# The local term of a Runge-Kutta step's first stage in two halves, with one prepared row between the two sums

## The chip, the cores and the metric

The kernel runs on one core of a Trainium2 chip. The metric is the device time of one execution in microseconds, the median of several executions. Of the engines, TensorE (PE in the profile, its weight loads PEld), VectorE (DVE) and ScalarE (ACT) carry the work; GpSimd (POOL) and the DMA queues have little to do.

## The reference

A sequence model in two parts. A recurrence with 256 time steps makes one state vector `q` of 512 values for each of 8 batch rows; each step is a classic four-stage Runge-Kutta step whose derivative holds a cube and a 512 x 512 product. The trace of `q` then goes through a gated feed-forward network with 4-bit weights, is normalised, and is added to the input.

```python
def _derivative(q, p, drive, coupling, bias):
    i_couple = jnp.tanh(q) @ coupling.T
    dq = q - q ** 3 / 3.0 - p + drive + i_couple + bias
    dp = EPSILON * (q + ALPHA - BETA * p)
    return (dq, dp)

def _rk4_step(q, p, drive, coupling, bias):
    dq1, dp1 = _derivative(q, p, drive, coupling, bias)
    dq2, dp2 = _derivative(q + 0.5 * DT * dq1, p + 0.5 * DT * dp1, drive, coupling, bias)
    dq3, dp3 = _derivative(q + 0.5 * DT * dq2, p + 0.5 * DT * dp2, drive, coupling, bias)
    dq4, dp4 = _derivative(q + DT * dq3, p + DT * dp3, drive, coupling, bias)
    ...

w_gu = _dequant_fp4(gate_up_packed, gate_up_scales, GROUP_SIZE)
w_down = _dequant_fp4(down_packed, down_scales, GROUP_SIZE)
gate_up = jnp.einsum('bsh,oh->bso', x, w_gu)
gate, up = (gate_up[..., :I], gate_up[..., I:])
h = jax.nn.silu(gate) * up
y = jnp.einsum('bsi,hi->bsh', h, w_down)
rms = jnp.sqrt(jnp.mean(y * y, axis=-1, keepdims=True) + EPS)
return y / rms
```

## The kernel before

The 512 values of `q` lie as 128 partitions x 4 chunks x 8 batch rows, so an operation on all of `q` has 32 elements in each partition and one on half of it (chunks 0 and 1, or 2 and 3) has 16. The 256 steps are cut into 16 blocks of 16 steps. A block's four stages per step make 64 stages; `s` counts them, and `s % 4` is the stage within the step (0 to 3).

One stage is a loop through four engines, written out by hand and held together by semaphores alone:

- ScalarE (L558, L560) makes the hyperbolic tangent of each half of the stage's `q` twice, once rounded to 16 bits (`th`) and once in 32 bits (`t32`, in the profile `t`): four instructions, half 0 first.
- VectorE (L592, `low_part`) subtracts the two, which gives the low 16 bits of `th`. I call the two of a stage low 0 and low 1.
- TensorE (L520) runs 32 matmuls of `th` with the coupling weights. The first 4 wait for half 0 of the rounded tangent, the 9th for half 1 (`tanh_hi`), the 13th for low 0 and the 21st for low 1 (`tanh_lo`). The 24th signals `first_half`, the 32nd `second_half`.
- VectorE makes `q_sq` (L596) and `q_cub` (L599), and from them the local term, which is all of the derivative that needs no product. `local_in` (L604) writes it into two of the six slots of the PSUM tile `scan_ps`: one slot belongs to half 0 of the sum, one to half 1. The other four slots are TensorE's. `finish` then sums three slots for each half (L628 and L630, which I call sum 0 and sum 1), and gives the next stage's `q`. ScalarE starts the next stage as soon as sum 0 is done.

The local term of stage `i` uses a row that is linear in the earlier stages' values. These rows are built up ahead by `add_q` and `add_p` (L586): `with_q1[0]` is used in stage 1, `with_q1[1]` goes into `with_q2[0]` late in stage 1, for stage 2. VectorE's queue is in order, so each of these stands at a fixed place between the others:

```python
                local_in(s)
                add_q(with_q1[1], 2, BY_Q1, q1, with_p[:, 2])
                finish(s)

                s = 4 * t + 1
                ffn_part(s)
```

The feed-forward network of a block is computed during the block behind it. A plan (`Schedule`) gives TensorE 132 products (L297 and L309, in the trace two records each) over the 64 stages: two behind each stage's 32 matmuls, but three behind stage 0 of the steps 0, 4, 8 and 12. VectorE has the network's element-wise work only at the head of a stage 1 (`ffn_part`): in a full block `ffn_h32` (L325) in the steps 0, 2, 3, 5, 6, 8, 9, 10, 12, 13 and 15, a third of `norm_out` (L346) in the steps 4, 7 and 11, and nothing in the steps 1 and 14. Block 0 has no network beside it, and block 1 has 10 of the `ffn_h32` (not that of step 0) and no `norm_out`. The last block's network runs in a tail behind the recurrence.

Of the kernel before, what the change touches and what calls it, by code (L numbers as in the profile page):

```python
# [21 lines left out]
ALU = mybir.AluOpType  # L22
# [8 lines left out]
HC = KT // 2  # L31
# [34 lines left out]
BY_R, BY_P, BY_Q1, BY_Q2, BY_Q3, BY_Q4, BY_ONE = range(7)  # L66
# [30 lines left out]
UNIT = [1.0] + [row_unit(i) for i in range(1, ROWS)]  # L97
# [103 lines left out]
def program(nc, x, drive, cond_t, coupling_t, bias_t, packed, scales, out):  # L201
    ctx = ExitStack()

    def sb(name, shape, dt=F32):
        return ctx.enter_context(nc.sbuf_tensor(name, shape, dt))
# [4 lines left out]
    with ctx:  # L210
# [12 lines left out]
        q_cub = sb("q_cub", [P, KT, B])  # L223
# [3 lines left out]
        with_p = sb("with_p", [P, ROWS, KT, B])  # L227
        with_q1 = [sb(f"with_q1_{i}", [P, KT, B]) for i in (1, 2, 3)]
# [33 lines left out]
        local_ps = scan_ps[:, 2 * APART:4 * APART].rearrange("p (h r) -> p h r", h=2)[:, :, 0:HB]  # L262

        def halves(tile):

            return tile.rearrange("p (h c) b -> p h (c b)", h=2)
# [306 lines left out]
        def dve_block(dve, now, before, ffn, rest):  # L573

            linear = [with_p[:, 0], with_q1[0][:, :, :], with_q2[0][:, :, :], with_q3[:, :, :]]
            count = [0]

            def local(ins):

                count[0] += 1  # L580
                ins.then_inc(now.local, 1)
                return count[0]

            def add(to, x, factor, base):

                return local(nc.vector.scalar_tensor_tensor(to, x, factor, base, ALU.mult, ALU.add))  # L586

            def low_part(s, half):

                c = slice(half * HC, (half + 1) * HC)  # L590
                dve.wait_ge(now.tanh_32, 2 * s + 1 + half)
                nc.vector.tensor_tensor(th[s % 2][:, c, 1, :], t32[:, c, :], th[s % 2][:, c, 0, :],  # L592
                                        ALU.subtract).then_inc(now.tanh_lo, 1)

            def square(i, q):
                return local(nc.vector.scalar_tensor_tensor(q_sq[:, :, :], q, CUBE[i], q, ALU.mult, ALU.mult))  # L596

            def cube(i, q):
                return local(nc.vector.scalar_tensor_tensor(q_cub[:, :, :], q_sq[:, :, :], OWN[i], q,  # L599
                                                            ALU.add, ALU.mult))  # L600

            def local_in(s):
                i = s % 4
                nc.vector.scalar_tensor_tensor(local_ps, halves(linear[i]), UNIT[i], halves(q_cub[:, :, :]),  # L604
                                               ALU.mult, ALU.add).then_inc(now.first_half, 1)

            def add_p(step, first, rows):
                p_rows = p_state[:, :, :].unsqueeze(1).to_broadcast([P, rows, KT, B])
                return add(with_p[:, first:first + rows], p_rows, P_ALL, sum_r[:, step % STEPS, first:first + rows])

            def add_q(to, row, column, q, base):
                return add(to[:, :, :], q, float(BY[row, column]), base)

            def clip(to, signal):
                nc.vector.tensor_scalar(to, q_raw[:, :, :], -CLAMP * S, CLAMP * S, ALU.max, ALU.min).then_inc(signal, 1)

            def ffn_part(s):

                for job in jobs(now, before, ffn, rest, s):
                    dve_ffn(dve, *job)  # L620

            def finish(s):

                i = s % 4
                q_next = q_raw if i == 3 else q_stage[i]

                dve.wait_ge(now.first_half, 2 * s + 2)
                nc.vector.tensor_reduce(q_next[:, 0:HC, :], three[0], AX.X, ALU.add).then_inc(now.q_ready, 1)  # L628
                dve.wait_ge(now.second_half, s + 1)
                nc.vector.tensor_reduce(q_next[:, HC:KT, :], three[1], AX.X, ALU.add).then_inc(now.q_ready, 1)  # L630

            for t in range(STEPS):
                q1 = hist[now.parity][:, :, t - 1, :] if t else hist[1 - now.parity][:, :, STEPS - 1, :]
                q2, q3, q4 = (x[:, :, :] for x in q_stage)

                s = 4 * t
                if t == STEPS - 1 and before:
                    dve.wait_ge(now.other_cleared, 1)
                if t == 0 and before:
                    dve.wait_ge(before.local, LOCALS)  # L640
                add_p(t, 1, 2)
                if t == 1 and rest:
                    dve.wait_ge(before.gu_ready, UNITS)
                if t:
                    dve.wait_ge(now.q_ready, 2 * s)
                    clip(q1, now.clipped)
                elif before:
                    dve.wait_ge(before.q_ready, 2 * STAGES)
                    clip(q1, before.clipped)
                low_part(s, 0)  # L650
                if t:
                    dve.wait_ge(now.clipped, t)
                elif before:
                    dve.wait_ge(before.clipped, STEPS)
                squared = square(0, q1)
                low_part(s, 1)
                dve.wait_ge(now.local, squared)
                cubed = cube(0, q1)
                add_q(with_q1[0], 1, BY_Q1, q1, with_p[:, 1])
                dve.wait_ge(now.local, cubed)  # L660
                local_in(s)
                add_q(with_q1[1], 2, BY_Q1, q1, with_p[:, 2])
                finish(s)

                s = 4 * t + 1
                ffn_part(s)
                dve.wait_ge(now.q_ready, 2 * s)
                squared = square(1, q2)
                low_part(s, 0)
                dve.wait_ge(now.local, squared)  # L670
                cubed = cube(1, q2)
                low_part(s, 1)
                dve.wait_ge(now.local, cubed)
                local_in(s)
                add(p_part[0][:, :, :], p_state[:, :, :], P_SUM[0], q1)
                add_q(with_q2[0], 2, BY_Q2, q2, with_q1[1][:, :, :])
                row3 = add_p(t, 3, 1)
                finish(s)

                s = 4 * t + 2  # L680
                dve.wait_ge(now.local, row3)
                add_q(with_q1[2], 3, BY_Q1, q1, with_p[:, 3])
                dve.wait_ge(now.q_ready, 2 * s)
                squared = square(2, q3)
                low_part(s, 0)
                dve.wait_ge(now.local, squared)
                cubed = cube(2, q3)
                low_part(s, 1)
                dve.wait_ge(now.local, cubed)
                local_in(s)  # L690
                p2 = add(p_part[1][:, :, :], p_part[0][:, :, :], P_SUM[1], q2)
                with_23 = add_q(with_q2[1], 3, BY_Q2, q2, with_q1[2][:, :, :])
                dve.wait_ge(now.local, p2)
                add(p_part[2][:, :, :], p_part[1][:, :, :], P_SUM[2], q3)
                finish(s)

                s = 4 * t + 3
                dve.wait_ge(now.local, with_23)
                add_q(with_q3, 3, BY_Q3, q3, with_q2[1][:, :, :])
                dve.wait_ge(now.q_ready, 2 * s)  # L700
                squared = square(3, q4)
                low_part(s, 0)
                p4 = add(p_part[3][:, :, :], p_part[2][:, :, :], P_SUM[3], q4)
                low_part(s, 1)
                dve.wait_ge(now.local, squared)
                cubed = cube(3, q4)
                dve.wait_ge(now.local, p4)
                p_next = local(nc.vector.tensor_scalar(p_state[:, :, :], p_part[3][:, :, :],  # L708
                                                       (-CLAMP - P_SHIFT) * S / P_UNIT, (CLAMP - P_SHIFT) * S / P_UNIT,
                                                       ALU.max, ALU.min))  # L710
                dve.wait_ge(now.local, cubed)
                local_in(s)
                if t + 1 == HS:
                    dve.wait_ge(now.sum_r_ready, SUM_R_PARTS)
                if t + 1 == STEPS:
                    dve.wait_ge(now.sum_r_ready, 2 * SUM_R_PARTS)
                dve.wait_ge(now.local, p_next)
                add_p(t + 1, 0, 1)
                finish(s)
            assert count[0] == LOCALS  # L720
# [132 lines left out]
```

## Time and profile before

| | before |
|---|---|
| median of 3 runs | 1509.6 us (1509.55 to 1509.95) |
| the profiled execution's own time | 1508.73 us |
| its span | 1506.8 us |
| TensorE, VectorE, ScalarE busy | 94%, 96%, 48% of the span |

The recurrence runs from about 64.5 us to 1468.7 us of the span; before it lie the loads and the unpacking of the weights, behind it the tail. The granted TensorE clock is full nearly throughout (0.999 of full speed over the span). A busy share says how long an engine had some instruction under way. VectorE's instructions overlap here (the next starts before the last has ended), so what counts is the distance from start to start, which the timeline shows.

### The profile page before, as it was taken

What the parts mean: (1) busy time and instruction counts of PE and PEld (TensorE: products, weight loads), DVE (VectorE), ACT (ScalarE), POOL (GpSimd) and SP (SyncE); (2) the same over time, 40 slices, a digit from 0 to 9 for tenths busy, and PEclk for the clock granted to TensorE, in tenths of its full rate; (3) what the DMA queues carried; (4) which work ended last, traced back from release to release, by engine and by line L of the source; (5) the groups of instructions that cost most, each with busy time, mean ns of one, the idle gap of its engine ahead of it and who ended that gap; (6) DMA issues with size and microseconds to landing.
All of it is one profiled execution on the core that took longest, in us unless ns stands there. A gap on an engine that the chain in (4) does not pass through costs nothing.

```text
span 1506.8 us, 90757 instructions
## 1 busy us (share of the span) xinstructions
PE 1413.9 (94%) x36992; PEld 1395.7 (93%) x36992; DVE 1450.1 (96%) x11277; ACT 718.9 (48%) x4836; POOL 12.2 (1%) x38
## 2 busy tenths in 40 slices
PE   0277999999999999999999999999999999999998
PEld 0166999999999999999999999999999999999998
DVE  6999999999999999999999999999999999999991
ACT  2144454545454554545454555545445455544541
POOL 0000000000000000000000000000000000000000
PEclk9999999999999999999999999999999999999999
DMA  9500000000000000000000000000000000000000
GB/s 250 135 7 3 15 8 7 4 25 4 21 8 22 7 4 25 4 22 7 22 8 4 25 4 23 6 21 7 5 25 4 25 4 22 7 4 25 4 21 22
DMA packets 13524, 32.70 MB, mean 22 GB/s; under 512 B 1712, under 2 KB 6064, under 8 KB 12976
## 3 DMA queue, kind: packets, MB, share of 16 engines
q1 hardware_dynamic: 13104, 26.89, 6.8%
q8 instruction: 289, 4.73, 1.3%
q14 instruction: 131, 1.07, 0.2%
HBM read 22.69 MB, written 4.19 MB: 18 GB/s over the span
## 4 chain that ended last, share of the span: by engine, by line
PE 87%; DVE 8%; issue 0%; ACT 0%; POOLq 0%; DVEq 0%; POOL 0%; ACTq 0%
PE scan_ps L520 51%; PE gu_ps L297 22%; PE y_ps L309 14%; DVE th L592 1%; DVE q_stage L630 1%; DVE with_q L586 1%; DVE q_sq L596 1%; DVE scan_ps L604 1%; DVE q_stage L628 1%; DVE q_cub L599 1%; DVE p_part L586 1%; DVE with_p L586 0%; DVE q_raw L630 0%; DVE q_raw L628 0%; DVE p_state L708 0%
## 5 line engine op out<-in xcount | busy, mean ns | idle before, releaser
L520 PE MATMUL scan_ps<-th,wscan 128*128 128x32 f16 (+1 forms) x32768 | 1005.9, 175 | 86.8 <-ACT th L558 86.3
L520 PEld LDWEIGHTS scan_ps<-th,wscan 128*128 128x128 f16 x32768 | 923.7, 96 | 104.4 <-ACT th L558 94.5
L558 ACT ACTIVATE th<-q_stage 128x16 f16<-128x16 f32 x1536 | 318.9, 208 | 525.0 <-DVE q_stage L628 525.0
L297 PE MATMUL gu_ps<-hist,wffn 128*128 128x128 f32 x2816 | 503.3, 284 | 0.0
L297 PEld LDWEIGHTS gu_ps<-hist,wffn 128*128 128x128 f32 x2816 | 393.9, 192 | 0.0
L592 DVE TENSOR_TENSOR th<-t,th 128x16 f16<-128x16 f32 x2048 | 357.0, 174 | 0.6 <-ACT t L560 0.2
L309 PE MATMUL y_ps<-wffn,h 128*128 128x128 f32 x1408 | 323.6, 313 | 0.0
L560 ACT ACTIVATE t<-q_stage 128x16 f32<-128x16 f32 x1536 | 306.1, 199 | 0.0
L309 PEld LDWEIGHTS y_ps<-wffn,h 128*128 128x128 f32 x1408 | 209.5, 189 | 0.4 <-DVE h L325 0.4
L558 ACT ACTIVATE th<-q_raw 128x16 f16<-128x16 f32 x512 | 106.2, 207 | 213.0 <-DVE q_raw L628 175.2
L375 ACT ACTIVATE sum_r<-dr,constant 128x64 f32<-128x64 f32 x528 | 174.2, 333 | 7.4 <-DMA dr<-drive 7.4
L628 DVE TENSOR_REDUCE q_stage<-scan_ps 128x16 f32<-128x48 f32 x768 | 158.3, 206 | 5.3 <-PE scan_ps L520 0.9
L630 DVE TENSOR_REDUCE q_stage<-scan_ps 128x16 f32<-128x48 f32 x768 | 159.4, 208 | 0.3
L604 DVE SCALAR_TENSOR_TENSOR scan_ps<-with_q,q_cub 128x32 f32<-128x32 f32 x768 | 153.4, 200 | 0.0
L586 DVE SCALAR_TENSOR_TENSOR with_p<-p_state,sum_r 128x32 f32<-128x32 f32 (+1 forms) x768 | 149.7, 195 | 0.6 <-PEq L395 0.3
L596 DVE SCALAR_TENSOR_TENSOR q_sq<-q_stage 128x32 f32<-128x32 f32 x768 | 145.1, 189 | 1.7
L586 DVE SCALAR_TENSOR_TENSOR p_part<-p_part,q_stage 128x32 f32<-128x32 f32 x768 | 143.6, 187 | 0.0
L599 DVE SCALAR_TENSOR_TENSOR q_cub<-q_sq,q_stage 128x32 f32<-128x32 f32 x768 | 143.4, 187 | 0.0
L586 DVE SCALAR_TENSOR_TENSOR with_q<-hist,with_p 128x32 f32<-128x32 f32 x768 | 141.0, 184 | 0.0
L586 DVE SCALAR_TENSOR_TENSOR with_q<-q_stage,with_q 128x32 f32<-128x32 f32 x768 | 140.9, 183 | 0.0
L560 ACT ACTIVATE t<-q_raw 128x16 f32<-128x16 f32 x512 | 102.0, 199 | 0.0
L325 DVE SCALAR_TENSOR_TENSOR h<-gu_ps,silu 128x128 f32<-128x128 f32 x176 | 49.5, 281 | 23.2 <-ACT silu L318 23.2
(33 smaller groups left out, 535.5 us busy)
## 6 DMA issues: line engine op xcount, KB each, us to landing
raw<-packed SPq DMA_DIRECT2D x11, 768.0 KB, 8.6
dr<-drive SPq DMA_DIRECT2D x34, 128.0 KB, 3.2
sc<-scales SPq DMA_DIRECT2D x11, 384.0 KB, 9.0
xres<-x SPq DMA_DIRECT2D x16, 256.0 KB, 3.7
out<-osb SPq DMA_DIRECT2D x16, 256.0 KB, 2.9
coup<-coupling_t SPq DMA_DIRECT2D x1, 1024.0 KB, 14.5
q_raw<-cond_t SPq DMA_DIRECT2D x1, 16.0 KB, 1.9
bias<-bias_t SPq DMA_DIRECT2D x1, 2.0 KB, 1.7
```

What stands on the lines that cost most here:

```text
L297: i = nc.tensor.matmul(gu_ps[b][:, half * P:(half + 1) * P], wffn[:, u, j * P:(j + 1) * P], hist[1 - f.parity][:, kt].rearrange("p t b -> ...
L309: i = nc.tensor.matmul(y_ps[f.parity][:, cols], h32[b][:, :], wffn[:, u, 2 * KT * P:][:, cols], start=(u == 0 and j == 0), stop=(u == UNIT ...
L375: nc.scalar.activation(sum_r[:, steps, row, c, :], dr[:, steps, c, :], ACT.Identity, bias=constant[:, row, c:c + 1], scale=float(BY[row, B ...
L520: i = nc.tensor.matmul(to if both else to[:, 0], wscan[:, w, part, kt, cols], moving if both else moving[:, 0], start=first, stop=last, sk ...
L558: nc.scalar.activation(th[s % 2][:, c, 0, :], q[:, c, :], ACT.Tanh, scale=1.0 / S).then_inc(now.tanh_hi, 1)
L560: nc.scalar.activation(t32[:, c, :], q[:, c, :], ACT.Tanh, scale=1.0 / S).then_inc(now.tanh_32, 1)
L586: return local(nc.vector.scalar_tensor_tensor(to, x, factor, base, ALU.mult, ALU.add))
L592: nc.vector.tensor_tensor(th[s % 2][:, c, 1, :], t32[:, c, :], th[s % 2][:, c, 0, :], ALU.subtract).then_inc(now.tanh_lo, 1)
L596: return local(nc.vector.scalar_tensor_tensor(q_sq[:, :, :], q, CUBE[i], q, ALU.mult, ALU.mult))
L604: nc.vector.scalar_tensor_tensor(local_ps, halves(linear[i]), UNIT[i], halves(q_cub[:, :, :]), ALU.mult, ALU.add).then_inc(now.first_half, 1)
L628: nc.vector.tensor_reduce(q_next[:, 0:HC, :], three[0], AX.X, ALU.add).then_inc(now.q_ready, 1)
L630: nc.vector.tensor_reduce(q_next[:, HC:KT, :], three[1], AX.X, ALU.add).then_inc(now.q_ready, 1)
```

## The change

In stage 0 of each of the 256 steps the single `local_in` (32 elements per partition) becomes two `local_half` of 16 elements. Half 0 signals `first_half` as before, half 1 signals `second_half`. The `add_q` that makes `with_q1[1]` and stood behind `local_in` moves between sum 0 and sum 1. Sum 1 now waits on a count of `second_half` that includes half 1's signal in each stage 0. The other three stages keep `local_in`, and their order is unchanged.

```diff
+            def local_half(s, half, signal):
+                i = s % 4
+                c = slice(half * HC, (half + 1) * HC)
+                nc.vector.scalar_tensor_tensor(local_ps[:, half], linear[i][:, c].rearrange("p c b -> p (c b)"),
+                                               UNIT[i], q_cub[:, c].rearrange("p c b -> p (c b)"),
+                                               ALU.mult, ALU.add).then_inc(signal, 1)
...
-            def finish(s):
+            def finish(s, between=None):
...
                 nc.vector.tensor_reduce(q_next[:, 0:HC, :], three[0], AX.X, ALU.add).then_inc(now.q_ready, 1)
-                dve.wait_ge(now.second_half, s + 1)
+                if between:
+                    between()
+
+                dve.wait_ge(now.second_half, s + 1 + s // 4 + 1)
                 nc.vector.tensor_reduce(q_next[:, HC:KT, :], three[1], AX.X, ALU.add).then_inc(now.q_ready, 1)
...
-                local_in(s)
-                add_q(with_q1[1], 2, BY_Q1, q1, with_p[:, 2])
-                finish(s)
+                local_half(s, 0, now.first_half)
+                local_half(s, 1, now.second_half)
+                finish(s, lambda: add_q(with_q1[1], 2, BY_Q1, q1, with_p[:, 2]))
```

VectorE's queue before, from the local term of a stage 0 to low 1 of the stage 1 behind it, in a step with an `ffn_h32` (`scan_ps` is the local term, `with_q1_2` the row that moves):

```order
L604 SCALAR_TENSOR_TENSOR scan_ps<-with_p,q_cub 128x2x16 [waits local_odd]
L586 SCALAR_TENSOR_TENSOR with_q1_2<-hist1,with_p 128x32
L628 TENSOR_REDUCE q_stage2<-scan_ps 128x16 [waits first_half_odd]
L630 TENSOR_REDUCE q_stage2<-scan_ps 128x16 [waits second_half_odd]
L325 SCALAR_TENSOR_TENSOR h32_0<-gu_ps0,silu0 128x128 [waits down_done_odd,silu_ready_odd]
L596 SCALAR_TENSOR_TENSOR q_sq<-q_stage2 128x32 [waits q_ready_odd]
L592 TENSOR_TENSOR th1<-t32,th1 128x2x8 [waits tanh_32_odd]
L599 SCALAR_TENSOR_TENSOR q_cub<-q_sq,q_stage2 128x32 [waits local_odd]
L592 TENSOR_TENSOR th1<-t32,th1 128x2x8 [waits tanh_32_odd]
```

The same place with the change:

```order
L610 SCALAR_TENSOR_TENSOR scan_ps<-with_p,q_cub 128x16 [waits local_odd]
L610 SCALAR_TENSOR_TENSOR scan_ps<-with_p,q_cub 128x16
L635 TENSOR_REDUCE q_stage2<-scan_ps 128x16 [waits first_half_odd]
L586 SCALAR_TENSOR_TENSOR with_q1_2<-hist1,with_p 128x32
L640 TENSOR_REDUCE q_stage2<-scan_ps 128x16 [waits second_half_odd]
L325 SCALAR_TENSOR_TENSOR h32_1<-gu_ps1,silu1 128x128 [waits down_done_odd,silu_ready_odd]
L596 SCALAR_TENSOR_TENSOR q_sq<-q_stage2 128x32 [waits q_ready_odd]
L592 TENSOR_TENSOR th1<-t32,th1 128x2x8 [waits tanh_32_odd]
L599 SCALAR_TENSOR_TENSOR q_cub<-q_sq,q_stage2 128x32 [waits local_odd]
L592 TENSOR_TENSOR th1<-t32,th1 128x2x8 [waits tanh_32_odd]
```

One row more stands ahead of sum 0 only in number: the row `with_q1_2` has left that place and now stands ahead of sum 1 and of all that follows it. Nothing moves on TensorE, ScalarE, GpSimd or the DMA queues.

## Rows read from the trace of the kernel before

**Rows 1.** The page, part 1: busy time and share, instructions.

```profile
PE 1413.9 (94%) x36992; PEld 1395.7 (93%) x36992; DVE 1450.1 (96%) x11277; ACT 718.9 (48%) x4836; POOL 12.2 (1%) x38
```

**Rows 2.** The list of waits: us in total, times, longest.

```profile
ACT th L558 <- DVE q_stage L628: 525.0, 768, 1.3
```

**Rows 3.** Timeline, a step with ffn_h32: start us, us, engine, line.

```profile
1151.87 0.20 DVE L604 SCALAR_TENSOR_TENSOR scan_ps<-with_p,q_cub 128x32 f32<-128x32 f32 x1
1151.97 0.18 DVE L586 SCALAR_TENSOR_TENSOR with_q<-hist,with_p 128x32 f32<-128x32 f32 x1
...
1152.10 0.21 DVE L628 TENSOR_REDUCE q_stage<-scan_ps 128x16 f32<-128x48 f32 x1
1152.28 0.21 DVE L630 TENSOR_REDUCE q_stage<-scan_ps 128x16 f32<-128x48 f32 x1
...
1152.34 0.22 ACT L558 ACTIVATE th<-q_stage 128x16 f16<-128x16 f32 x1 [0.84 <-DVE q_stage L628]
...
1152.40 0.28 DVE L325 SCALAR_TENSOR_TENSOR h<-gu_ps,silu 128x128 f32<-128x128 f32 x1
1152.47 0.20 ACT L560 ACTIVATE t<-q_stage 128x16 f32<-128x16 f32 x1
...
1152.60 0.18 DVE L596 SCALAR_TENSOR_TENSOR q_sq<-q_stage 128x32 f32<-128x32 f32 x1
1152.61 0.90 PEld L520 LDWEIGHTS scan_ps<-th,wscan 128*128 128x128 f16 x32
...
1152.68 0.20 ACT L560 ACTIVATE t<-q_stage 128x16 f32<-128x16 f32 x1
1152.70 0.17 DVE L592 TENSOR_TENSOR th<-t,th 128x16 f16<-128x16 f32 x1
...
1152.92 0.17 DVE L592 TENSOR_TENSOR th<-t,th 128x16 f16<-128x16 f32 x1
...
1153.15 0.18 DVE L586 SCALAR_TENSOR_TENSOR p_part<-p_state,hist 128x32 f32<-128x32 f32 x1
...
1153.46 0.20 DVE L628 TENSOR_REDUCE q_stage<-scan_ps 128x16 f32<-128x48 f32 x1
```

**Rows 4.** Groups by form: count, busy us, mean ns of one, idle before.

```profile
L592 DVE TENSOR_TENSOR th<-t,th 128x16 f16<-128x16 f32 x2048 | 357.0, 174 | 0.6 <-ACT t L560 0.2
...
L586 DVE SCALAR_TENSOR_TENSOR with_p<-p_state,sum_r 128x32 f32<-128x32 f32 x512 | 94.6, 185 | 0.3 <-issue 0.3
L586 DVE SCALAR_TENSOR_TENSOR with_p<-p_state,sum_r 128x64 f32<-128x64 f32 x256 | 55.1, 215 | 0.3 <-PEq L395 0.3
...
L604 DVE SCALAR_TENSOR_TENSOR scan_ps<-with_p,q_cub 128x32 f32<-128x32 f32 x256 | 51.4, 201 | 0.0
```

**Rows 5.** Timeline, a step with nothing of the network on VectorE.

```profile
1196.03 0.21 DVE L628 TENSOR_REDUCE q_stage<-scan_ps 128x16 f32<-128x48 f32 x1
...
1196.20 0.21 DVE L630 TENSOR_REDUCE q_stage<-scan_ps 128x16 f32<-128x48 f32 x1
...
1196.39 0.20 ACT L560 ACTIVATE t<-q_stage 128x16 f32<-128x16 f32 x1
1196.44 0.19 DVE L596 SCALAR_TENSOR_TENSOR q_sq<-q_stage 128x32 f32<-128x32 f32 x1
...
1196.63 0.17 DVE L592 TENSOR_TENSOR th<-t,th 128x16 f16<-128x16 f32 x1
```

**Rows 6.** Timeline, step 8 of a block, three products and ffn_h32.

```profile
1163.80 0.96 PE L520 MATMUL scan_ps<-th,wscan 128*128 128x16 f16 x32
1163.89 0.17 DVE L592 TENSOR_TENSOR th<-t,th 128x16 f16<-128x16 f32 x1
```

**Rows 7.** Timeline, step 4 of a block, three products and norm_out.

```profile
1141.67 0.20 ACT L560 ACTIVATE t<-q_stage 128x16 f32<-128x16 f32 x1
...
1141.83 0.96 PE L520 MATMUL scan_ps<-th,wscan 128*128 128x16 f16 x32
...
1142.03 0.17 DVE L592 TENSOR_TENSOR th<-t,th 128x16 f16<-128x16 f32 x1
```

## The prediction

> **What bounds the kernel now.** I read the page first: TensorE 94% and VectorE 96% busy [rows 1]. Neither number says which of them holds the end, since both are sums of overlapping records. The list of waits shows the loop itself: ScalarE waited 768 times for sum 0 of a stage, 525.0 us in all [rows 2]. So the time is 1024 turns of one loop, sum 0 to tangent to TensorE to sum 0, and I read one turn in the timeline, in a step with `ffn_h32` [rows 3]. Times below are counted from the start of sum 0 of stage 0 (1152.10), which I call zero.
>
> - ScalarE starts at 0.24: sum 0 takes 0.21, and 0.03 pass from its end to the start of what waited for it. This 0.03 to 0.04 between two engines, or between two dependent VectorE instructions, comes back everywhere.
> - TensorE's weight load for stage 1 starts at 0.51, which is the tangent's end (0.24 + 0.22) plus 0.05. It came straight from its wait: in this step TensorE is not the bound, though the page calls it busy.
> - ScalarE's 32-bit tangents end at 0.57 and 0.78. Low 0 starts at 0.60, low 1 at 0.82. Low 0 is thus due at the same moment by two roads: ScalarE (0.57 + 0.03), and VectorE's own queue, sum 1 at 0.18, `h` at 0.30, `q_sq` at 0.50, low 0 0.10 later. `q_sq` at 0.50 came straight behind `h`, not behind a wait: sum 1 ended at 0.39. Low 1 lies 0.01 behind ScalarE's road (0.78 + 0.03), so there VectorE's queue rules.
> - Low 1 releases TensorE's 21st matmul. 32 matmuls of which each takes about 0.176 start over 0.96 - 0.176 [rows 6], so one starts every 0.025. Low 1's end at 0.99, plus 0.05 to 0.07 to TensorE, plus three starts, plus 0.176, plus 0.04 gives about 1.35: sum 0 of stage 1 stands at 1.36 [rows 3]. So whatever delays low 1 of a stage 1 delays the loop by as much.
>
> At the head of this, in stage 0, sum 0 at zero starts 0.03 behind the end of the local term (-0.23 + 0.20) and 0.13 behind the row `with_q`. TensorE would have allowed it earlier: sum 1 at 0.18 waits for the 32nd matmul, the 24th is eight starts (0.20) ahead of that, so sum 0 could stand at -0.02 to -0.03.
>
> **The change, part by part.**
>
> *Half 0 instead of the whole local term.* It starts where the whole one did, since it waits for the same cube. Its duration isn't in the trace. An operation of 64 elements takes 215 ns and one of 32 takes 185 [rows 4], about 0.94 ns an element, so 16 elements less give 201 - 15 = 186. The 16-element operation there is, low, takes 174 against 185 for 32, 11 less, which gives 190. I take 187: sum 0 comes 0.014 earlier. Bounds: nothing (the half takes as long as the whole) and 0.025 (TensorE's limit above).
>
> *Half 1 added.* By the same rows it starts under 0.10 behind half 0 and ends some 0.28 behind half 0's start. It stands in the shadow of sum 0's wait, which lasts to half 0's end (0.22), and sum 1 comes far behind it. Cost nothing; if that cover were gone, 0.09 a step.
>
> *The row moved between the sums.* Ahead of sum 0 its removal gives nothing beyond the 0.014, since sum 0 waited for the local term anyway. Behind sum 0 it must be paid. From a sum to the next instruction are 0.12 (sum 1 at 1152.28, `h` at 1152.40). From a row to the next instruction is a third of 1153.15 to 1153.46, three starts, 0.103 [rows 3]. So sum 1 stands 0.12 + 0.103 = 0.223 behind sum 0, where now it stands 0.175 behind (0.18 and 0.17 [rows 3, 5]), when TensorE lets it go. The idle place between the sums is 0.05 long and the row needs 0.10. Sum 1 comes 0.048 - 0.014 = 0.034 later. Bounds: with the 0.025 for sum 0 and 0.11 instead of 0.12, it is 0.013; with no gain at sum 0 and 0.01 more, 0.058.
>
> *Who waits for sum 1.* Behind it on VectorE's queue stand `h` or `osb`, `q_sq`, low 0, cube, low 1. In steps with network work at the head of stage 1 the whole queue was tight, so low 0 and low 1 come 0.034 later, and with them the loop. In the 28 such steps with `norm_out`, VectorE was already the later road: low 1 starts 0.16 behind the end of ScalarE's second tangent [rows 7].
>
> In a step with no network work [rows 5], `q_sq` stands 0.24 behind sum 1, which is sum 1's 0.21 and the 0.03. Low 0 could follow at 0.10, at 1196.54, but starts at 1196.63, where ScalarE's road (1196.39 + 0.20 + 0.03) lets it. That cover of 0.09 takes all of the 0.034, and the loop keeps the 0.014 of sum 0. ScalarE's second half needs sum 1 too: its end at 0.223 + 0.21 + 0.03 = 0.46 stands just ahead of where ScalarE's queue would start it (its 32-bit tangent of half 1 at 1152.68, less one spacing of 0.11, is 0.47). That cover is 0.01.
>
> In the steps 0, 4, 8 and 12 TensorE has three products and starts stage 1's matmuls late. Low 1 ends at 1164.06 [rows 6], 0.07 more makes 1164.13, and the 21st matmul starts at 1163.80 + 20 x 0.025 = 1164.30: slack 0.17. With `norm_out` it is 1142.20 + 0.07 against 1142.33 [rows 7]: slack 0.06. Both swallow 0.034, and an earlier sum 0 gives nothing either. These 60 steps (15 blocks) don't change.
>
> *The sum.* Of 256 steps: block 0 has 16 and block 1 four with no network work and two products, and the 14 full blocks two each, 48 in all. `ffn_h32` without a third product: 8 a block, 15 blocks, 120. `norm_out` without: steps 7 and 11 of 14 blocks, 28. The rest is 60. So (120 + 28) x 0.034 = +5.0 us, 48 x 0.014 = -0.7 us, and 60 x 0 = 0: +4.3 us. The profiled execution took 1508.73 us (span 1506.8), which gives 1513.0; the median of the runs stands 0.9 above that execution, so 1509.6 + 4.3 = 1513.9 us.
>
> **A rule weighed.** Three rows on VectorE start 0.10 apart though each takes 0.18 [rows 3], so the next one starts before the last has ended. The Trainium skill, "VectorE: DVE Perf Modes", section "The DRAIN you can't avoid", says the next operation doesn't start until the pipe is empty (with a remark that one that isn't held starts earlier); it speaks against any row put between the sums. What it would make of the time is the fourth rival.
>
> **The rivals.**
>
> 1. *Faster: the tangents hide the late sum 1 everywhere.* If low 0 and low 1 of the `ffn_h32` and `norm_out` steps waited for ScalarE with cover as they have it in a step without network work [rows 5], all 196 steps outside the 60 would gain 0.014: 2.7 us, 1506.9; with TensorE's limit 0.025, 1504.7. It decides where ScalarE's road is more than 0.034 behind VectorE's. For it: low 0 sits exactly 0.03 behind ScalarE [rows 3]. Against: `q_sq` came straight behind `h`, and low 1 lies behind ScalarE by 0.01 already. Chance 0.06.
> 2. *TensorE absorbs it.* If the products' backlog carried the loop outside the 60 steps too, as the page's 94% suggests, nothing would change: 1509.6. Against: the weight load starts right behind the tangent [rows 3]. A milder form belongs here: at the lower bound, 148 x 0.013 - 48 x 0.025 = +0.7, 1510.3. Chance 0.13.
> 3. *The half isn't shorter.* Sum 0 gains nothing, sum 1 comes 0.048 to 0.058 later: 148 x 0.048 to 0.058 = +7.1 to +8.6 us, 1516.7 to 1518.2. For it: more than half of these short operations' time doesn't depend on size. Chance 0.13.
> 4. *No overlap behind sum 0.* Sum 0, row and sum 1 end to end put sum 1 at 0.21 + 0.18 = 0.39, 0.20 later than the wait does now: about 148 x 0.20 = 30 us, and 1 to 3 us more where it exceeds the slacks of 0.17 and 0.06, some 1541. The rows contradict it. Chance 0.02.
>
> **How the numbers follow.** Forecast 0.66, the rivals 0.06, 0.13, 0.13 and 0.02. The likeliest case runs from 1511.9 to 1516 (shift of sum 1 between 0.02 and 0.048). The range 1511.0 to 1517.8 takes in most of the third rival and the upper part of the second, and leaves out 1, 4 and the exact no-change. A change under 0.2% (3.0 us, up to 1512.6) can't be told from none: that takes the second rival, and 0.06 of the forecast where its shift is smallest. So faster 0.06, same 0.19, slower 0.75.
>
> **What the profile will show.** Right: in stage 0, half 0 at about 187 ns and sum 0 0.03 behind its end; from sum 0 to sum 1 0.22 to 0.23 in all steps; low 1 of stage 1 in the `ffn_h32` steps 0.03 behind its place before, against sum 0 0.05 behind; steps without network work shorter by 0.014; steps with a third product unchanged. Wrong, if the distance between the sums stayed at 0.18, if low 1 still stood at 0.82 behind sum 0 in `ffn_h32` steps, or if TensorE's first weight load of stage 1 came later than 0.05 behind the tangent in them.

## The result, and the profile after

| | before | changed |
|---|---|---|
| median | 1509.55 us (17 runs, 1508.99 to 1511.16) | 1512.77 us (17 runs, 1512.05 to 1513.63) |
| ratio | | 1.0021, 95% interval 1.0014 to 1.0029 |
| profiled execution, own time | 1508.73 us | 1512.77 us |
| its span | 1506.8 us | 1511.0 us |

The change makes the kernel slower by 3.2 us, 0.21%. It is small, but its interval is clear of 1. The forecast was +4.3 us.

The page after, its span and its busy times, which answer to [rows 1]:

```profile
span 1511.0 us, 91013 instructions
...
PE 1417.4 (94%) x36992; PEld 1401.5 (93%) x36992; DVE 1454.9 (96%) x11533; ACT 720.4 (48%) x4836; POOL 12.2 (1%) x38
```

And the list of waits after, the row that answers to [rows 2]:

```profile
ACT th L558 <- DVE q_stage L635: 526.6, 768, 1.4
```

Neither shows what happened: the shares are the same, VectorE has 256 instructions more (one half a step), and ScalarE waits as it did. The reader has to go to one turn of the loop. The timeline of the changed kernel at the same step as in [rows 3] (a step with `ffn_h32`):

```profile
1155.12 0.27 DVE L610 SCALAR_TENSOR_TENSOR scan_ps<-with_p,q_cub 128x16 f32<-128x16 f32 x2
...
1155.35 0.21 DVE L635 TENSOR_REDUCE q_stage<-scan_ps 128x16 f32<-128x48 f32 x1
...
1155.47 0.18 DVE L586 SCALAR_TENSOR_TENSOR with_q<-hist,with_p 128x32 f32<-128x32 f32 x1
...
1155.57 0.20 DVE L640 TENSOR_REDUCE q_stage<-scan_ps 128x16 f32<-128x48 f32 x1
1155.59 0.22 ACT L558 ACTIVATE th<-q_stage 128x16 f16<-128x16 f32 x1 [0.82 <-DVE q_stage L635]
...
1155.69 0.28 DVE L325 SCALAR_TENSOR_TENSOR h<-gu_ps,silu 128x128 f32<-128x128 f32 x1
...
1155.85 0.94 PEld L520 LDWEIGHTS scan_ps<-th,wscan 128*128 128x128 f16 x32
...
1155.88 0.18 DVE L596 SCALAR_TENSOR_TENSOR q_sq<-q_stage 128x32 f32<-128x32 f32 x1
1155.92 0.20 ACT L560 ACTIVATE t<-q_stage 128x16 f32<-128x16 f32 x1
1155.98 0.17 DVE L592 TENSOR_TENSOR th<-t,th 128x16 f16<-128x16 f32 x1
...
1156.21 0.17 DVE L592 TENSOR_TENSOR th<-t,th 128x16 f16<-128x16 f32 x1
...
1156.74 0.20 DVE L635 TENSOR_REDUCE q_stage<-scan_ps 128x16 f32<-128x48 f32 x1
```

Just ahead of sum 0 VectorE's queue still has two instructions: now the two halves, before the local term and the row. Counted from sum 0: the row starts 0.12 behind it and sum 1 0.22 behind it, where before sum 1 stood at 0.18. `h` comes 0.12 behind sum 1 and `q_sq` 0.19 behind `h`, as before. Low 0 stands at 0.63 and low 1 at 0.86, before at 0.60 and 0.82; ScalarE's last tangent ends at 0.77, so low 1 no longer has anything to do with it. Sum 0 of stage 1 is at 1.39 instead of 1.36. TensorE's first weight load of stage 1 starts at 0.50, 0.04 behind the tangent's end; over all `ffn_h32` steps it is 0.05 in both kernels.

One road into TensorE is missing from the description of the kernel before: the 5th matmul of a stage waits for sum 1 itself (`q_ready`). It doesn't bind here. In the `ffn_h32` steps the 5th matmul starts 0.21 behind the end of sum 1 on average, before 0.25, and a weight load starts 0.05 behind what it waits for.

The same in a step with no network work on VectorE, which answers to [rows 5]:

```profile
1199.41 0.21 DVE L635 TENSOR_REDUCE q_stage<-scan_ps 128x16 f32<-128x48 f32 x1
...
1199.63 0.20 DVE L640 TENSOR_REDUCE q_stage<-scan_ps 128x16 f32<-128x48 f32 x1
...
1199.77 0.20 ACT L560 ACTIVATE t<-q_stage 128x16 f32<-128x16 f32 x1
1199.87 0.19 DVE L596 SCALAR_TENSOR_TENSOR q_sq<-q_stage 128x32 f32<-128x32 f32 x1
...
1200.00 0.17 DVE L592 TENSOR_TENSOR th<-t,th 128x16 f16<-128x16 f32 x1
```

Sum 1 is as late as in the other step, but low 0 stands at 0.59 (before 0.60), 0.03 behind the end of ScalarE's tangent: the late sum 1 is covered. And in step 8 of a block, with its third product, which answers to [rows 6]:

```profile
1167.11 0.96 PE L520 MATMUL scan_ps<-th,wscan 128*128 128x16 f16 x32
...
1167.22 0.17 DVE L592 TENSOR_TENSOR th<-t,th 128x16 f16<-128x16 f32 x1
```

The 21st matmul starts at 1167.11 + 20 x 0.025 = 1167.61, low 1 ends at 1167.39: 0.15 left after the 0.07 to TensorE, where 0.17 were.

Timeline rows have steps of 10 ns, and the terms here are smaller. So I took the starts of all 1024 sums 0 from both traces and averaged their distances by kind of step (changed minus before, in ns). "Stage 3 to 0" is the distance from sum 0 of the stage 3 in front to sum 0 of stage 0, and so on. Ahead of that I set apart single stops: distances over 0.12 us longer than the same place has in the median of the blocks.

| kind of step | steps | stage 3 to 0 | stage 0 to 1 | stages 1 to 3 | a step | all, us |
|---|---|---|---|---|---|---|
| `ffn_h32`, two products | 120 | -16.6 | +44.2 | -2.4 | +25 | +3.04 |
| `norm_out`, two products | 28 | -18.1 | +42.1 | +3.5 | +27 | +0.77 |
| no network work, blocks 1 to 15 | 32 | -16.8 | +4.8 | -0.2 | -12 | -0.39 |
| block 0 | 16 | -0.5 | +6.6 | +0.1 | +6 | +0.10 |
| third product | 60 | -15.9 | +16.0 | +0.6 | +1 | +0.04 |
| single stops | | | | | | -0.40 |

The sum is +3.16 us, and the medians differ by 3.2. The two spans differ by 4.2; of that, 1.0 lies before the first sum 0 (65.4 us into the span before, 66.4 after), where the change does nothing.

The changed kernel was traced a second time (the run "the change once more" below). There the kinds of step add up to +2.6 us instead of +3.6: `ffn_h32` +22 ns a step, `norm_out` +24, no network work -17, block 0 nothing, third product -3. So two executions of the same kernel differ by 3 to 6 ns a step, and a term of that size, as block 0's +6, can't be told from nothing. That +3.16 meets the 3.2 of the medians so closely is in part chance.

### The profile page after: what moved, and what is told of

The parts are those of the page before. It is cut to its first block, busy times and chain, and to the rows that moved or that the text cites. A ratio compares the mean times of both kernels' runs of the same rounds, so it can differ in the third digit from the quotient of the medians.

```text
span 1511.0 us, 91013 instructions
## 1 busy us (share of the span) xinstructions
PE 1417.4 (94%) x36992; PEld 1401.5 (93%) x36992; DVE 1454.9 (96%) x11533; ACT 720.4 (48%) x4836; POOL 12.2 (1%) x38
## 4 chain that ended last, share of the span: by engine, by line
PE 86%; DVE 9%; issue 0%; ACT 0%; POOLq 0%; DVEq 0%; POOL 0%; ACTq 0%
PE scan_ps L520 50%; PE gu_ps L297 22%; PE y_ps L309 14%; DVE th L592 1%; DVE with_q L586 1%; DVE q_stage L640 1%; DVE q_sq L596 1%; DVE q_stage L635 1%; DVE q_cub L599 1%; DVE p_part L586 1%; DVE scan_ps L604 1%; DVE with_p L586 1%; DVE scan_ps L610 0%; DVE q_raw L640 0%; DVE q_raw L635 0%; DVE hist L622 0%
```

## The experiments

Each experiment was timed beside the kernel before on its own chip, and the ratios and differences are against those runs. Where I give nanoseconds by kind of step, they are against the one trace of the kernel before, with single stops set apart. That execution took 1508.73 us, 1.0 more than the median of before beside the first four experiments, so they show the pattern and don't add up to the measured difference.

**The two parts of the change, each alone.** First the halves without the move:

```diff
                 local_half(s, 0, now.first_half)
                 local_half(s, 1, now.second_half)
-                finish(s, lambda: add_q(with_q1[1], 2, BY_Q1, q1, with_p[:, 2]))
+                add_q(with_q1[1], 2, BY_Q1, q1, with_p[:, 2])
+                finish(s)
```

> The local term in two halves as in the change, but the row stays ahead of sum 0. My theory: half 0, half 1 and the row start 0.09 and 0.10 us apart, so sum 0 can start only 0.05 us later than in the kernel before, while sum 1 still starts when TensorE lets it (0.175 behind the old sum 0). The ScalarE road then is 0.05 late: steps without network work +0.05 each (48), ffn_h32 steps +0.035 each (120, their VectorE queue had 0.015 of lead over it), norm_out steps and steps with a third product 0. Together 6.5 us over the kernel before. If only the place of sum 1 mattered (rival), it would equal the kernel before.

Measured: 1512.83 against 1507.75 us, ratio 1.0032 (1.0020 to 1.0045), +5.1 us. Its timeline in the step with `ffn_h32`:

```profile
1155.27 0.27 DVE L610 SCALAR_TENSOR_TENSOR scan_ps<-with_p,q_cub 128x16 f32<-128x16 f32 x2
1155.45 0.18 DVE L586 SCALAR_TENSOR_TENSOR with_q<-hist,with_p 128x32 f32<-128x32 f32 x1
...
1155.55 0.20 DVE L635 TENSOR_REDUCE q_stage<-scan_ps 128x16 f32<-128x48 f32 x1
1155.68 0.21 DVE L640 TENSOR_REDUCE q_stage<-scan_ps 128x16 f32<-128x48 f32 x1
```

Sum 0 stands 0.28 behind the local term's start instead of 0.23, by the number of instructions in front of it alone: the two halves take 0.18 of the queue. Averaged over the steps it is 0.042 later, not 0.050. The `ffn_h32` steps lose 21 ns each, not 35, and those without network work 27, not 50: which steps pay was right, what they pay was set too high. The rival (only sum 1 counts) falls: sum 1 keeps its place against the old one and the kernel is slower. So the halves alone lose against the kernel before. That they lose more than the whole change isn't shown: the intervals overlap, and in the traces the recurrence, from its first sum 0 to its last, takes 1406.2 us in this kernel and 1406.3 and 1405.3 in the two of the changed one.

Then the move without the halves:

```diff
-                local_half(s, 0, now.first_half)
-                local_half(s, 1, now.second_half)
+                local_in(s)
                 finish(s, lambda: add_q(with_q1[1], 2, BY_Q1, q1, with_p[:, 2]))
```

> The whole local term as before, only the row moved between the two sums. My theory: sum 0 stays, sum 1 comes 0.049 us later, and 148 steps pay 0.043 each of it: 6.4 us over the kernel before, so about 3 us slower than the change. If the split gives nothing (rival), it equals the change, 3.2 us over the kernel before.

Measured: 1514.01 against 1507.75 us, ratio 1.0041 (1.0027 to 1.0054), +6.3 us.

```profile
1156.13 0.20 DVE L604 SCALAR_TENSOR_TENSOR scan_ps<-with_p,q_cub 128x32 f32<-128x32 f32 x1
...
1156.37 0.21 DVE L635 TENSOR_REDUCE q_stage<-scan_ps 128x16 f32<-128x48 f32 x1
...
1156.49 0.18 DVE L586 SCALAR_TENSOR_TENSOR with_q<-hist,with_p 128x32 f32<-128x32 f32 x1
...
1156.59 0.20 DVE L640 TENSOR_REDUCE q_stage<-scan_ps 128x16 f32<-128x48 f32 x1
```

So the move alone costs 6.3 us, 4.1 to 8.1 by its interval, where the change cost 3.2. By the medians the halves give 3.1 us back, each kernel taken against its own runs of before, but these two intervals overlap. The traces put it lower: the recurrence takes 1407.9 us here against 1406.3 and 1405.3 in the changed kernel, so 1.6 to 2.5 us. Sum 0 comes 13 to 15 ns earlier with the halves in `ffn_h32` steps. The Trainium skill, "Perfetto Trace Analysis", section "Optimizing Scalar/DVE Operations", says that breaking up instructions may let work finish sooner where VectorE isn't saturated but holds another engine up. VectorE is 96% busy here by the page of the profile, so the condition is not plainly met; the gain of 13 to 15 ns at sum 0, for which ScalarE waits, has the sign that the section gives, and the first experiment shows the other side of it.

**No row at all.**

```diff
-                finish(s, lambda: add_q(with_q1[1], 2, BY_Q1, q1, with_p[:, 2]))
+                finish(s)
...
-                add_q(with_q2[0], 2, BY_Q2, q2, with_q1[1][:, :, :])
+                add_q(with_q2[0], 2, BY_Q2, q2, with_p[:, 2])
```

> The local term in two halves and the row left out altogether (stage 2's linear term lacks its q1 part, so the computation is not the reference's). Sum 0 comes 0.016 to 0.020 us earlier, sum 1 stays with TensorE. My theory: in steps with network work VectorE's queue behind sum 1 sets low 1, so only the 48 steps without it gain: 0.8 to 1.0 us below the kernel before. If ScalarE's road sets the loop in all steps (rival), 196 steps gain: 3.1 to 3.9 us below.

Measured: 1507.30 against 1507.75 us, ratio 0.9996 (0.9987 to 1.0005). The rival's 3.1 us or more lie outside that interval. The timeline:

```profile
1151.67 0.21 DVE L635 TENSOR_REDUCE q_stage<-scan_ps 128x16 f32<-128x48 f32 x1
...
1151.87 0.21 DVE L640 TENSOR_REDUCE q_stage<-scan_ps 128x16 f32<-128x48 f32 x1
...
1151.99 0.28 DVE L325 SCALAR_TENSOR_TENSOR h<-gu_ps,silu 128x128 f32<-128x128 f32 x1
...
1152.51 0.17 DVE L592 TENSOR_TENSOR th<-t,th 128x16 f16<-128x16 f32 x1
```

With nothing between the sums, sum 1 stands 0.20 behind a sum 0 that comes earlier, that is, where TensorE lets it go. Low 1 stands 0.64 behind sum 1, as before (0.82 - 0.18). In such a step an earlier sum 0 is worth next to nothing by itself, because the queue behind sum 1 is the later road: averaged, sum 0 of stage 0 came 20 ns earlier and that of stage 1 only 2. With 5 ns more in the later stages `ffn_h32` steps gained 7 ns, those without network work in blocks 1 to 15 gained 23, and block 0 nothing.

**The row twice.** The change with a second copy of the row, into a tile that nobody reads.

> The change with the row computed twice between the sums, the second into a tile nobody reads. My theory: sum 1 comes 0.103 us later still; 148 steps pay 0.103 each (15.2 us), the 48 steps without network work now pay 0.10 too, since ScalarE's second half waits for sum 1 (4.7 us), the 14 third-product steps with norm_out 0.09 (1.2 us), the 44 with ffn_h32 nothing (slack 0.17): 21 us above the change, 24 over the kernel before. If TensorE absorbed delays of sum 1 (rival 2), 10 us or less above the change.

Measured: 1531.64 against 1507.75 us, ratio 1.0156 (1.0142 to 1.0170), +23.9 us.

```profile
1170.17 0.21 DVE L636 TENSOR_REDUCE q_stage<-scan_ps 128x16 f32<-128x48 f32 x1
...
1170.29 0.18 DVE L587 SCALAR_TENSOR_TENSOR with_q<-hist,with_p 128x32 f32<-128x32 f32 x1
...
1170.39 0.18 DVE L587 SCALAR_TENSOR_TENSOR spare<-hist,with_p 128x32 f32<-128x32 f32 x1
...
1170.49 0.20 DVE L641 TENSOR_REDUCE q_stage<-scan_ps 128x16 f32<-128x48 f32 x1
...
1170.72 0.21 ACT L559 ACTIVATE th<-q_stage 128x16 f16<-128x16 f32 x1
```

Each row costs 0.10 of the queue, and ScalarE's second half now starts 0.23 behind sum 1's start, 0.03 behind its end, in steps of every kind: it waits for it. By kind of step against the trace of before: `ffn_h32` +120 ns, `norm_out` +118, no network work +82, block 0 +100, third product with `norm_out` +51, with `ffn_h32` -1. This is the pattern of covers that the prediction took from the rows: 0.17 of slack swallowed even two rows.

**The change once more, only in the steps where it gains, and in another stage.** The three kernels ran beside the changed kernel on one chip.

> The changed kernel once more, beside the runs of the kernel before on the same chip and beside the three kernels that follow. 3.1 us over the kernel before, which is what the stages of its trace add up to: 148 steps with network work and two products pay 0.025 each, 48 without network work gain 0.015.

Measured: 1512.37 against 1509.12 us, ratio 1.0022 (1.0014 to 1.0031), +3.3 us.

```diff
+                if any(at in plan.h32 or at in plan.norm_out for plan, _, _, at in jobs(now, before, ffn, rest, s + 1)):
+                    local_in(s)
+                    add_q(with_q1[1], 2, BY_Q1, q1, with_p[:, 2])
+                    finish(s)
+                else:
+                    local_half(s, 0, now.first_half)
+                    local_half(s, 1, now.second_half)
+                    finish(s, lambda: add_q(with_q1[1], 2, BY_Q1, q1, with_p[:, 2]))
```

> The change only in the 50 steps whose stage 1 has no network work on VectorE; the other 206 have the old order. My theory: only the gain is left, 48 x 0.015 = 0.7 us below the kernel before, 3.8 us below the change. If the split brought its gain in the other steps (rival), it would lose by this and stand above the kernel before.

Measured: 1509.15 against 1509.12 us, ratio 1.0000 (0.9991 to 1.0009). The loss is gone; the expected 0.7 us gain is smaller than what this measurement can tell. In the trace 32 of the 48 steps are 12 ns shorter, block 0's 16 are unchanged, and so are the network steps within 2 ns: 0.4 us in all, of the size of the scatter between two traces. What the run does show is that the loss sits in the steps with network work: leaving them alone took 3.2 us off the changed kernel's time.

Stage 3 with the same edit (stage 0 as before):

```diff
-                local_in(s)
+                local_half(s, 0, now.first_half)
+                local_half(s, 1, now.second_half)
...
-                add_p(t + 1, 0, 1)
-                finish(s)
+                    add_p(t + 1, 0, 1)
+
+                finish(s, row0)
```

> Stage 0 as before; the same edit in stage 3 instead: the local term in two halves, and the row for the next step (add_p of row 0) between the two sums. In stage 3 sum 0 waits for the local term too, 0.012 us longer than for TensorE. Behind sum 1 low 0 of the next stage waits for ScalarE with 0.048 us to spare on VectorE's queue, and ScalarE's second half with 0.03, so the late sum 1 (0.022) should cost nothing. My theory: all 256 steps gain 0.012, 3.1 us below the kernel before. If a row between the sums costs wherever it stands (rival), 256 x 0.02 = 5 us above it.

Measured: 1507.05 against 1509.12 us, ratio 0.9984 (0.9975 to 0.9993), -2.1 us. It is faster, but not for the reason I gave alone. The end of stage 3 in step 7 of a block, before:

```profile
1160.99 0.33 ACT L375 ACTIVATE sum_r<-dr,constant 128x64 f32<-128x64 f32 x1
...
1161.43 0.20 DVE L604 SCALAR_TENSOR_TENSOR scan_ps<-with_q,q_cub 128x32 f32<-128x32 f32 x1
1161.59 0.19 DVE L586 SCALAR_TENSOR_TENSOR with_p<-p_state,sum_r 128x32 f32<-128x32 f32 x1
...
1161.70 0.20 DVE L628 TENSOR_REDUCE q_raw<-scan_ps 128x16 f32<-128x48 f32 x1
```

and in this kernel:

```profile
1160.60 0.27 DVE L611 SCALAR_TENSOR_TENSOR scan_ps<-with_q,q_cub 128x16 f32<-128x16 f32 x2
...
1160.83 0.21 DVE L637 TENSOR_REDUCE q_raw<-scan_ps 128x16 f32<-128x48 f32 x1
...
1160.95 0.18 DVE L587 SCALAR_TENSOR_TENSOR with_p<-p_state,sum_r 128x32 f32<-128x32 f32 x1
```

In the steps 7 and 15 `add_p` has a second wait in front of it, for ScalarE's `sum_r`. ScalarE had long been done: this `sum_r` ended at 1161.32, 0.27 ahead of the row, and in step 15 the last one ended 1.61 ahead. In the trace the extra wait is an instruction of VectorE's sequencer (L717, 32 of them, 21 ns each), and behind it the row starts 0.16 behind the local term, where it starts 0.11 behind it in the other steps. Before, that held sum 0 up: 0.27 behind the local term, now 0.23. These two steps gained 0.045 and 0.044 in stage 3 (medians of the blocks), some 30 steps, 1.3 us. The others gained about 0.012 in stage 3 and gave part of it back, since low 1 of their stage 1 came 9 ns later behind sum 0. No run takes these two parts of the 2.1 us apart.

> Both together: the edit in stage 3 of all steps, and in stage 0 of the 50 steps without network work on VectorE. The two should add up: 3.1 + 0.7 = 3.8 us below the kernel before. If the gain in stage 3 is lost (rival), 0.7 below or slower.

Measured: 1507.06 against 1509.12 us, ratio 0.9983 (0.9974 to 0.9992), -2.1 us. It equals the kernel before it in this list; whether the 0.7 us are there can't be told.

**The row in another stage.** After these I tried to keep the early sum 0 without paying for the row:

```diff
-                finish(s, lambda: add_q(with_q1[1], 2, BY_Q1, q1, with_p[:, 2]))
+                finish(s)
...
                 local_in(s)
+                row2 = add_q(with_q1[1], 2, BY_Q1, q1, with_p[:, 2])
                 add(p_part[0][:, :, :], p_state[:, :, :], P_SUM[0], q1)
-                add_q(with_q2[0], 2, BY_Q2, q2, with_q1[1][:, :, :])
                 row3 = add_p(t, 3, 1)
-                finish(s)
+
+                def second_row2():
+                    dve.wait_ge(now.local, row2)
+                    add_q(with_q2[0], 2, BY_Q2, q2, with_q1[1][:, :, :])
+
+                finish(s, second_row2)
```

> Stage 0 keeps the two halves but holds no row behind them: the row is made in stage 1 behind the local term, and the row that stage 1 made there (with_q2[0]) goes between stage 1's two sums. So VectorE has as many instructions ahead of each sum 0 of stage 1 as before, and the row between sums stands where the queue behind it has 0.05 us to spare (low 0 of stage 2 waits for ScalarE). My theory: sum 1 of stage 1 comes 0.025 later and costs nothing, sum 0 of stage 0 comes 0.016 to 0.020 earlier and sum 1 of stage 0 stays with TensorE, so the steps gain what the run without the row showed, 0.007 with network work and 0.015 without: 1.2 to 1.9 us below the kernel before. If a row between two sums costs wherever it stands (rival), 3 us or more above.

Measured: 1510.78 against 1509.44 us, ratio 1.0009 (1.0000 to 1.0017), +1.3 us. A miss: I expected 1.2 to 1.9 below. In `ffn_h32` steps sum 0 of stage 0 came 16 ns earlier, but that of stage 1 1 ns later, not 2 earlier as in the run without the row, and stages 1 to 3 became 6 ns longer: a row between the sums of stage 1 isn't free outside block 0 (there stages 1 to 3 kept their length), though the 0.05 us of cover were there. The rival's 3 us or more lie outside the interval, too. The expected gain, a few ns a step, was smaller than what such a move disturbs.

> The same, with the edit in stage 3 too. If both are independent they add up: 2.1 us (stage 3 alone, measured) and 1.2 to 1.9: 3.3 to 4.0 us below the kernel before. If the gain of stage 3 comes back in stage 1, where VectorE's queue in steps with network work is the later road (its low 1 was 0.009 later in that run), it stays at 2.1 to 2.5.

Measured: 1508.18 against 1509.44 us, ratio 0.9991 (0.9982 to 1.0000), -1.3 us, a miss as well: 3.3 to 4.0 below lies outside the interval, and the rival's 2.1 to 2.5 is only at its edge. Stage 3 gives 2.6 us against the kernel without it, but the pair is no better than stage 3 alone. Of all kernels, each against its own runs of before, those with stage 3's edit and stage 0's old order for network steps are the fastest.

## Why the prediction was right, point by point

**What bounds the kernel: shown.** The row left out and the row doubled moved the time as a loop with two roads into low 1 does, not as a busy share would. None of the three signs of being wrong came: the sums stand 0.22 apart, low 1 stands at 0.86 in `ffn_h32` steps, and TensorE's weight load still starts 0.05 behind the tangent.

**Half 0: right, sized a little low.** The group of the halves in the changed kernel:

```profile
L610 DVE SCALAR_TENSOR_TENSOR scan_ps<-with_p,q_cub 128x16 f32<-128x16 f32 x512 | 69.0, 180 | 0.0
```

180 ns is the mean over both halves. Half 0 alone takes 184 on average, against the 187 taken and the 201 of the whole term, so sum 0 came 17 ns earlier, not 14 (18 in the second trace of the same kernel).

**Half 1 costs nothing: right,** as long as the row isn't in front of sum 0 too (first experiment).

**Sum 1 0.034 later: right.** The distance between the sums went from 173.5 to 223.2 ns in `ffn_h32` steps, +50 where I had +48; less sum 0's 17 it is 33.

**Who pays: right in kind, the size off.** Low 1 in the `ffn_h32` steps came 27 ns later (43 behind sum 0, less 17), not 34. The 7 ns between lie at one place, which I took as fixed at 0.12: from sum 1 to the instruction behind it. It was 124.8 ns on average before and is 117.8 after, in the `norm_out` steps 125.0 and 117.6. Before, sum 1 had itself waited for TensorE; after, it starts straight behind the row. In the kernel without the row, where sum 1 waits again, it is 124.9. That ScalarE's road took up the delay, the other candidate, doesn't fit: in the `norm_out` steps low 0 lies 0.13 behind that road, and low 1 came as little late there (44 ns behind sum 0). With 2 ns given back in the later stages the term 148 x 0.034 = 5.0 us measured 3.04 + 0.77 = 3.8 us. This is most of the distance between +4.3 and +3.2 (in the second trace the term measured 3.3).

**48 x 0.014: wrong for a third of the steps.** The 32 outside block 0 gained 12 a step (17 in the second trace). That is near my 14, but by two errors against each other: sum 0 gained 17, and low 1 stands 6 ns later behind it, because ScalarE's fourth tangent does (last section). Block 0 gained nothing, in this kernel or in any other with the halves. I took it as one kind with the others, from rows of block 12. The timeline before in block 0:

```profile
91.97 1.04 PE L520 MATMUL scan_ps<-th,wscan 128*128 128x16 f16 x32 [0.34 <-ACT th L558]
...
92.58 0.20 DVE L604 SCALAR_TENSOR_TENSOR scan_ps<-with_p,q_cub 128x32 f32<-128x32 f32 x1
...
92.83 0.21 DVE L628 TENSOR_REDUCE q_stage<-scan_ps 128x16 f32<-128x48 f32 x1
```

In block 0 the 32 matmuls of stage 0 take 1.04, where they take 0.98 to 1.00 in the later blocks. They stand behind an idle stretch of 0.34 that the later blocks fill with products; why they take longer no run shows. So both roads reach sum 0 together there: before, it starts 37 ns behind the local term's end (elsewhere 34) and 37 behind the 24th matmul's, which is also the distance from the 32nd matmul to a sum 1 that waits for it. With the halves it starts 55 ns behind half 0's end and still 36 behind the 24th matmul: TensorE holds it. The term was -0.7 us and measured -0.3.

**60 steps unchanged: right,** +1 a step; the row twice left the `ffn_h32` ones unchanged too.

**What the sum couldn't hold.** The -0.40 us of single stops has no step in the prediction; that it brings the measured time down by an eighth of the change is luck (last section).

**The rivals.** The late sum 1 hidden everywhere falls by the sign of the result, and by the row left out, whose interval ends at 2.0 us of gain. TensorE as the cover: only in the 60 steps; its milder form, a smaller shift of sum 1, falls by the +50 ns between the sums. The half that isn't shorter: half 0 takes 184 ns against 201. No overlap behind sum 0: the row starts 0.12 behind sum 0, which takes 0.21. I had priced this rival at 30 us and a little more, and left out that the 48 steps without network work would pay too; in the run with the row twice they paid 0.08 to 0.10 each for a sum 1 that stood 0.33 behind sum 0. The Trainium skill, "VectorE: DVE Perf Modes", section "The DRAIN you can't avoid", says that the next operation waits for an empty pipe, with the remark that one that isn't held starts earlier; the trace shows these instructions as the remark has it, not as the rule.

## What to carry to other kernels

An idle place is worth the distance between the starts on both sides of it less what the first instruction needs (here 0.175 - 0.125 = 0.05), and a row that needs 0.10 there delays all that is queued behind it; ask of each kind of iteration, not of the average one, what else that queue would have waited for. An earlier start of one road is worth next to nothing where another road arrives later (here 2 of 20 ns), so look at both ends of a join before moving work from one to the other. Halving an instruction pays where something waits for its end, and costs where something waits for the queue.

## What the hardware showed that I had not expected

Single stops of VectorE that nothing in the program explains. In the changed kernel, in step 7 of block 9:

```profile
900.50 0.20 DVE L604 SCALAR_TENSOR_TENSOR scan_ps<-with_q,q_cub 128x32 f32<-128x32 f32 x1
901.02 0.19 DVE L586 SCALAR_TENSOR_TENSOR with_p<-p_state,sum_r 128x32 f32<-128x32 f32 x1 [0.31 <-issue]
```

The row starts 0.52 behind the local term instead of the 0.16 of other steps 7, and the loop loses 0.35 us. The kernel before has three such losses of 0.26 to 0.36 us (blocks 3, 5 and 10), 0.97 us in all; the changed one two, 0.56 us. (Both have two more in step 0 of block 1, the same in every kernel.) They aren't chance: the two experiments with as many VectorE instructions as the kernel before (11277: the whole term with the row moved, the halves without the row) have its three losses at the same places, and of the four further traces with 11533, as the change has, three have both of its places (the changed kernel again, the halves without the move, and the row in stage 1, which has two more losses) and the stage 3 kernel one of them and two others. What they are, no run tried; they moved this comparison by 0.4 us.

ScalarE's four tangents of a stage start at nearly fixed distances, unless one waits. The distance from the third to the fourth was 105.4 ns on average in stage 1 before and 110.7 after, though in both the third one started at its usual place. After the change sum 1 ended 45 ns ahead of the third tangent, before 90. The run with the edit in stage 3 has 110.8 in stage 0 (45.7 ns ahead), and the run with a row between the sums of stage 1 has 111.0 in stage 2 (45.7 ns ahead). The run with the whole term and the row moved has 110.6 in stage 1 (44.5 ns ahead). So a late producer cost the engine some 5 ns even where it didn't hold its start, in all of these places. Why, no run shows. In the steps without network work low 1 waits for the fourth tangent (33 ns behind its end before and after), so there the 5 to 6 ns reach the loop. It is also of the size of what the run with the row in stage 1 lost in the stages behind it; that it is the cause there was not tried.
